# The mean and variance of a group over the partitions: one rounded pass over a high and a low half in place of a float32 product

## The chip, the cores and the metric

The kernel runs on one core of a Trainium2 chip. The metric is the time of one execution on the device, in microseconds (us), lower is better; stated is the median of the runs.

## What is computed

Two attention layers run one after the other on 16 samples of 256 channels by 2048 positions. The first layer ends in a group norm with one group: mean and variance are taken over all channels and positions of a sample. Cut to what matters here:

```
# layer 0
q, k from y; v from x
attn = softmax(q k^T / sqrt(E))               # 32 x 32 per head, over all positions
o = Wo (attn v) + bo + x
mu  = mean(o, axis=(1, 2)); var = var(o, axis=(1, 2))      # one value per sample
x1  = (o - mu) * rsqrt(var + EPS) * gn_w + gn_b
# layer 1
u = Wo1 (softmax of chunks of 64 positions of y, masked) + b
z = u + x1
out = (z - mean(z, axis=2)) * rsqrt(var(z, axis=2) + EPS)  # per channel
```

## The kernel before

Channels lie on the 128 partitions in two halves; the positions of a sample are cut into four blocks of 512. The program is written out by hand for each engine: for every sample `n` there are 16 slots `s`, and each engine runs through the slots in the order of its own `body`, with semaphores between engines. Large products run in float32r (rounded): each operand is split into a high half, which is the value rounded, and a low half, which is the rest, and `three_pass` (L313) sums three rounded products. Other products, such as the transposes (L339), are plain float32, and the trace shows each of them as two weight loads and two matmuls.

The statistics of the group norm of sample `n` are taken while `o` is made, in slots 12 to 15 (`stats_of_o`). After slot 15 of sample `n`, and across slot 0 of sample `n + 1`, they are brought together; this stretch is called the sample boundary here, and there are 15 of them, and a last one in the tail of the program. The steps are:

1. VectorE: `group_mean` (L944, L945). bn_aggr gives a mean and a variance for each partition, `o_mv`. The small copy to `carrier` ahead of it stands between the last statistics and the aggregation.
2. TensorE: `mean_over_partitions` (L489). A 128x128 matrix of 1/128 times the column of means puts the mean over the partitions on every partition, in `l0_ps[0]`. It stands behind the scores (L328) and the value products (L357) of slot 0, and ahead of the query products (L313) of the next block.
3. VectorE: `group_deviation` (L950 to L953), behind `branch` (L876), `top` (L847) and `att_low` (L871): mean copied to `o_mu`, difference squared and added to the partition's variance, `o_dev`. Behind it stands the subtraction of the row maximum, `shift` (L854).
4. TensorE: `variance_over_partitions` (L493), behind twelve query products, ahead of the transposes of the probabilities (L339).
5. VectorE: `group_variance` (L957), behind `shift`. It adds EPS and sets `gn_step`.
6. GpSimd: `group_norm` (L1137 to L1143) makes scale and shift. TensorE: the first Gram product of the next sample (`gram_part`, L424) writes the same bank of PSUM, so it waits for `gn_step` too:

```
                if q == 0:
                    if exists(n - 1, 1, 0):
                        pe.wait_ge(gn_step, count(n - 1, 1, 0))
```

In the tail the same five functions run one behind the other for sample 15; there the output product of block 2 stands behind the variance's product, and VectorE's L1100 waits for `gn_done` of GpSimd.

Of the kernel before, what the change touches and what calls it, by code (L numbers as in the profile page):

```python
# [16 lines left out]
F32R = mybir.dt.float32r  # L17
BF16 = mybir.dt.bfloat16
ALU = mybir.AluOpType
# [35 lines left out]
def build(nc, x, ctx, ctx_t, mask, w0, w1, cols, bk0, consts, out):  # L55
# [6 lines left out]
    with es:  # L62
        def sb(name, shape, dt=F32):
            return es.enter_context(nc.sbuf_tensor(name, shape, dt))
# [15 lines left out]
        c1 = sb("c1", [P, HALVES])  # L80

# [46 lines left out]
        o_dev = sb("o_dev", [P, 2])  # L128
        o_var = sb("o_var", [P, 1])
# [52 lines left out]
        power_set = sem("power_set")  # L182
        c1_done = sem("c1_done")
# [122 lines left out]
        def _(pe):  # L306
# [180 lines left out]
            def mean_over_partitions(n):  # L487
                pe.wait_ge(o_aggr, count(n, 1, 0))
                mm(l0_ps[0][:, 0:1], mean_mat, o_mv[:, 0:1], start=True, stop=True).then_inc(mean_ready, 1)  # L489

            def variance_over_partitions(n):
                pe.wait_ge(dev_done, count(n, 1, 0))
                mm(l0_ps[0][:, 1:2], mean_mat, o_dev[:, 1:2], start=True, stop=True).then_inc(var_ready, 1)  # L493
# [90 lines left out]
        def _(act):  # L584
# [145 lines left out]
            split_yt(0, 0)  # L730
            act.wait_ge(w0_in, 2 * 16)
# [91 lines left out]
        def _(dve):  # L823
# [118 lines left out]
            def group_mean(n):  # L942
                dve.wait_ge(o_stats_done, count(n, 8, 7))
                nc.vector.tensor_copy(carrier[:, 0:1], ident[:, 0:1])  # L944
                nc.vector.bn_aggr(o_mv[:, :], o_stats[:, :, :].rearrange("p a b -> p (a b)")).then_inc(o_aggr, 1)  # L945

            def group_deviation(n):
                dve.wait_ge(mean_ready, count(n, 1, 0))
                dve.wait_ge(o_aggr, count(n, 1, 0))
                nc.vector.tensor_copy(o_mu[:, :], l0_ps[0][:, 0:1])  # L950
                tt(o_dev[:, 0:1], o_mv[:, 0:1], l0_ps[0][:, 0:1], ALU.subtract).then_inc(dev_step, 1)
                dve.wait_ge(dev_step, count(n, 1, 0))
                stt(out=o_dev[:, 1:2], in0=o_dev[:, 0:1], scalar=o_dev[:, 0:1], in1=o_mv[:, 1:2], op0=ALU.mult, op1=ALU.add).then_inc(dev_done, 1)  # L953

            def group_variance(n):
                dve.wait_ge(var_ready, count(n, 1, 0))
                nc.vector.tensor_scalar(o_var[:, :], l0_ps[0][:, 1:2], EPS, None, ALU.add).then_inc(gn_step, 1)  # L957
# [281 lines left out]
```

## Time and profile before

| | |
|---|---|
| median of 3 runs | 1543.38 us (1541.15 to 1543.43) |
| the profiled execution | 1542.93 us |
| its span in the trace | 1541.1 us |
| TensorE busy | 1511.2 us, 98% of the span |
| VectorE busy | 1278.6 us, 83% |
| ScalarE busy | 1108.9 us, 72% |
| GpSimd busy | 450.8 us, 29% |
| granted TensorE clock, mean | 0.995 of 2.4 GHz |

The profile comes from one execution. PE is TensorE's matmuls and PEld its weight loads, DVE is VectorE, ACT ScalarE, POOL GpSimd. A busy share is an average over the whole program; what an operation of a sample boundary is worth is read from the rows of that boundary. Times in the timeline are in us from the start of the span, with two decimals, so a difference of two rows is good to about 0.01 us.

### The profile page before, as it was taken

What the parts mean: (1) busy time and instruction counts of PE and PEld (TensorE: products, weight loads), DVE (VectorE), ACT (ScalarE), POOL (GpSimd) and SP (SyncE); (2) the same over time, 40 slices, a digit from 0 to 9 for tenths busy, and PEclk for the clock granted to TensorE, in tenths of its full rate; (3) what the DMA queues carried; (4) which work ended last, traced back from release to release, by engine and by line L of the source; (5) the groups of instructions that cost most, each with busy time, mean ns of one, the idle gap of its engine ahead of it and who ended that gap; (6) DMA issues with size and microseconds to landing.
All of it is one profiled execution on the core that took longest, in us unless ns stands there. A gap on an engine that the chain in (4) does not pass through costs nothing.

```text
span 1541.1 us, 54826 instructions
## 1 busy us (share of the span) xinstructions
PE 1511.2 (98%) x24146; PEld 1274.8 (83%) x24146; DVE 1278.6 (83%) x2024; ACT 1108.9 (72%) x2064; POOL 450.8 (29%) x294
## 2 busy tenths in 40 slices
PE   9999999999999999999999999999999999999995
PEld 6888888888888888888888888888888888888883
DVE  5778888888788887978879888888888889788897
ACT  6667676777767777677776776867767776777765
POOL 1114133141331413314142141422314133141321
PEclk9999999999999999999999999999999999999998
DMA  7232331423315233142422414233142331524212
GB/s 250 56 99 83 111 124 38 152 84 118 111 36 152 84 118 111 54 148 71 143 86 84 132 57 145 84 111 121 55 151 78 120 116 41 149 83 129 59 49 91
DMA packets 96397, 157.28 MB, mean 102 GB/s; under 512 B 5408, under 2 KB 38304, under 8 KB 96032
## 3 DMA queue, kind: packets, MB, share of 16 engines
q1 hardware_dynamic: 96160, 153.78, 31.8%
q8 instruction: 191, 3.13, 0.8%
q14 instruction: 46, 0.38, 0.1%
HBM read 120.20 MB, written 33.55 MB: 100 GB/s over the span
## 4 chain that ended last, share of the span: by engine, by line
PE 96%; DVE 1%; ACT 1%; issue 1%; POOL 0%; ACTq 0%; POOLq 0%; DVEq 0%
PE pj_ps L313 46%; PE l_ps L313 12%; PE s_ps L328 9%; PE w_ps L339 8%; PE l_ps L424 7%; PE w_ps L357 7%; PE l_ps L441 2%; PE l_ps L468 2%; PE l_ps L462 1%; PE l_ps L471 1%; PE s_ps L499 0%; PE l_ps L450 0%; DVE o_sb L972 0%; PE l_ps L432 0%; PE l_ps L489 0%
## 5 line engine op out<-in xcount | busy, mean ns | idle before, releaser
L1132 POOL TENSOR_TENSOR prob<-prob,row_inv 128x1024 f32<-128x1024 f32 x128 | 257.9, 2015 | 890.4 <-DVE row_inv L864 890.4
L671 ACT CAST att_hi<-w_ps 128x256 fp32r<-128x256 f32 x256 | 83.2, 380 | 192.2 <-PE w_ps L357 192.1
L313 PE MATMUL pj_ps<-y_hi,w_hi 128*128 128x512 f32 x510 | 207.4, 407 | 0.0
L313 PE MATMUL pj_ps<-y_hi,w_lo 128*128 128x512 f32 x510 | 202.0, 396 | 0.0
L313 PE MATMUL pj_ps<-y_lo,w_hi 128*128 128x512 f32 x510 | 202.0, 396 | 0.0
L859 DVE TENSOR_REDUCE row_sum<-prob 128x16 f32<-128x1024 f32 x128 | 155.0, 1211 | 49.2 <-ACT prob L640 49.1
L847 DVE TENSOR_REDUCE row_max<-s_ps 128x16 f32<-128x1024 f32 x128 | 155.6, 1215 | 21.2 <-PE s_ps L328 21.2
L328 PEld LDWEIGHTS s_ps<-k_s,q_s 32*64 32x64 f32 x8192 | 130.8, 133 | 43.1 <-issue 35.2
L1149 POOL TENSOR_TENSOR o_sb<-o_sb,u_sb 128x1024 f32<-128x1024 f32 x60 | 157.7, 2638 | 0.9
L854 DVE TENSOR_TENSOR prob<-s_ps,row_max 128x1024 f32<-128x1024 f32 x128 | 155.6, 1215 | 0.1
L635 ACT COPY prob_t<-w_ps 128x512 f32<-128x512 f32 x256 | 152.2, 596 | 3.8 <-PE w_ps L339 3.1
L832 DVE TENSOR_TENSOR yt_hl<-yt_raw,yt_hl 128x1024 fp32r<-128x1024 f32 x64 | 94.8, 1482 | 70.0 <-ACT yt_hl L603 70.0
L620 ACT ACTIVATE q_s<-pj_ps,col 128x512 f32<-128x512 f32 x128 | 88.3, 690 | 89.4 <-PE pj_ps L313 88.6
L313 PE MATMUL pj_ps<-w_hi,y_hi 128*128 128x256 f32 x512 | 150.4, 294 | 0.8 <-ACT v_s L631 0.8
L339 PE MATMUL w_ps<-cst,prob 128*128 128x128 f32 x1024 | 147.8, 275 | 1.4
L328 PE MATMUL s_ps<-k_s,q_s 32*64 32x64 f32 x8192 | 148.5, 220 | 0.0
L313 PE MATMUL pj_ps<-w_hi,y_lo 128*128 128x256 f32 x512 | 144.5, 282 | 0.0
L313 PE MATMUL pj_ps<-w_lo,y_hi 128*128 128x256 f32 x512 | 144.0, 281 | 0.0
L651 ACT COPY s_ps<-blocked 128x512 f32<-128x512 f32 x256 | 143.1, 603 | 0.0
L339 PEld LDWEIGHTS w_ps<-cst,prob 128*128 128x128 f32 x1024 | 118.5, 141 | 25.9 <-issue 12.0
L640 ACT ACTIVATE prob<-prob 128x1024 f32<-128x1024 f32 x128 | 137.8, 1076 | 1.8 <-DVE prob L854 1.6
L837 DVE TENSOR_TENSOR x_lo<-x_raw,x_hi 128x1024 fp32r<-128x1024 f32 x62 | 78.8, 1271 | 62.9 <-ACT x_hi L613 62.8
(139 smaller groups left out, 3552.2 us busy)
## 6 DMA issues: line engine op xcount, KB each, us to landing
y_raw<-in_ctx SPq DMA_DIRECT2D x64, 512.0 KB, 4.9
yt_raw<-in_ctx_t SPq DMA_DIRECT2D x64, 512.0 KB, 4.6
x_raw<-in_x SPq DMA_DIRECT2D x64, 512.0 KB, 5.1
out_z<-o_sb SPq DMA_DIRECT2D x60, 512.0 KB, 3.6
mask_b<-in_mask SPq DMA_DIRECT2D x64, 256.0 KB, 4.0
out_z<-o_sb SPq DMA_DIRECT2D x8, 256.0 KB, 2.7
u_sb<-in_w SPq DMA_DIRECT2D x2, 512.0 KB, 5.8
w_sb<-in_w SPq DMA_DIRECT2D x1, 1024.0 KB, 10.7
```

The source lines that it names most:

```text
L313: last = mm(dst, lhs, rhs, start=i == 0, stop=i == len(todo) - 1)
L328: last = mm(s_ps[64 * h:64 * h + 64, r, t // 2, g, t % 2, :], q_s[rows, b % 2, g, cut], k_s[rows, b % 2, g, cut], start=False, stop=True, ...
L339: last = nc.tensor.transpose(pt_ps[:, j, 2 * g + r, :], prob[:, u % 2, r, j, g, :], ident)
L357: last = mm(av_ps[DH * i:DH * i + DH, c, g, j, :], v_s[rows, b % 2, 2 * e + j, o:o + DH], prob_t[rows, j, g, i // 2, i % 2, :], start=True ...
L635: copy(prob_t[:, j].rearrange("p g r h q -> p (g r h q)"), w_ps[:, j, :]).then_inc(pt_copied, 1)
L640: nc.scalar.activation(cut, cut, ACT.Exp, scale=SCALE1).then_inc(exp_done, 1)
L651: last = copy(s_ps[:, r].rearrange("p j g c k -> p j g (c k)"), blocked[:, b % 2, e * UT:(e + 1) * UT].rearrange("p (j t) -> p j t", j=2). ...
L847: nc.vector.tensor_reduce(row_max[:, u % 2, :], s_ps[:, :, :, :, :, :].rearrange("p r j g c k -> p (r j g c) k"), AX.X, ALU.max).then_inc( ...
L854: tt(prob[:, u % 2].rearrange("p r j g (c k) -> p (r j g c) k", c=2), s_ps[:, :, :, :, :, :].rearrange("p r j g c k -> p (r j g c) k"), ro ...
L859: nc.vector.tensor_reduce(row_sum[:, u % 2, :], prob[:, u % 2].rearrange("p r j g (c k) -> p (r j g c) k", c=2), AX.X, ALU.add).then_inc(s ...
L1132: nc.gpsimd.tensor_tensor(cut, cut, row_inv[:, u % 2, :].unsqueeze(2).to_broadcast([P, 2 * HEADS, CHUNK]), ALU.mult).then_inc(probs_done, 1)
L1149: nc.gpsimd.tensor_tensor(o_sb[:, :, cut], o_sb[:, :, cut], u_sb[:, :, cut], ALU.add).then_inc(z_done, 1)
```

## The change

The two products over the partitions become one rounded pass each. The matrix of 1/128 is copied once to float32r (`mean_r`, on ScalarE). VectorE splits the column of means into a high and a low half (`mean_hl`), TensorE multiplies both columns in one matmul of two columns, and VectorE sums the two results with a reduce. The same is done for the variance (`dev_hl`). Each new operation on VectorE waits for the one ahead of it through a semaphore of its own.

```diff
             def mean_over_partitions(n):
-                pe.wait_ge(o_aggr, count(n, 1, 0))
-                mm(l0_ps[0][:, 0:1], mean_mat, o_mv[:, 0:1], start=True, stop=True).then_inc(mean_ready, 1)
+                pe.wait_ge(mean_split, count(n, 1, 0))
+                mm(l0_ps[0][:, 0:2], mean_r[:, :], mean_hl[:, :], start=True, stop=True).then_inc(mean_ready, 1)
 
             def variance_over_partitions(n):
-                pe.wait_ge(dev_done, count(n, 1, 0))
-                mm(l0_ps[0][:, 1:2], mean_mat, o_dev[:, 1:2], start=True, stop=True).then_inc(var_ready, 1)
+                pe.wait_ge(dev_split, count(n, 1, 0))
+                mm(l0_ps[0][:, 2:4], mean_r[:, :], dev_hl[:, :], start=True, stop=True).then_inc(var_ready, 1)
...
             split_yt(0, 0)
+            act.wait_ge(consts_in, 16)
+            copy(mean_r[:, :], mean_mat)
             act.wait_ge(w0_in, 2 * 16)
...
                 nc.vector.bn_aggr(o_mv[:, :], o_stats[:, :, :].rearrange("p a b -> p (a b)")).then_inc(o_aggr, 1)
+                dve.wait_ge(o_aggr, count(n, 1, 0))
+                nc.vector.tensor_copy(mean_hl[:, 0:1], o_mv[:, 0:1]).then_inc(mean_hi_done, 1)
+                dve.wait_ge(mean_hi_done, count(n, 1, 0))
+                tt(mean_hl[:, 1:2], o_mv[:, 0:1], mean_hl[:, 0:1], ALU.subtract).then_inc(mean_split, 1)
 
             def group_deviation(n):
                 dve.wait_ge(mean_ready, count(n, 1, 0))
-                dve.wait_ge(o_aggr, count(n, 1, 0))
-                nc.vector.tensor_copy(o_mu[:, :], l0_ps[0][:, 0:1])
-                tt(o_dev[:, 0:1], o_mv[:, 0:1], l0_ps[0][:, 0:1], ALU.subtract).then_inc(dev_step, 1)
+                nc.vector.tensor_reduce(o_mu[:, :], l0_ps[0][:, 0:2], AX.X, ALU.add).then_inc(mu_done, 1)
+                dve.wait_ge(mu_done, count(n, 1, 0))
+                tt(o_dev[:, 0:1], o_mv[:, 0:1], o_mu[:, :], ALU.subtract).then_inc(dev_step, 1)
                 dve.wait_ge(dev_step, count(n, 1, 0))
                 stt(out=o_dev[:, 1:2], in0=o_dev[:, 0:1], scalar=o_dev[:, 0:1], in1=o_mv[:, 1:2], op0=ALU.mult, op1=ALU.add).then_inc(dev_done, 1)
+                dve.wait_ge(dev_done, count(n, 1, 0))
+                nc.vector.tensor_copy(dev_hl[:, 0:1], o_dev[:, 1:2]).then_inc(dev_hi_done, 1)
+                dve.wait_ge(dev_hi_done, count(n, 1, 0))
+                tt(dev_hl[:, 1:2], o_dev[:, 1:2], dev_hl[:, 0:1], ALU.subtract).then_inc(dev_split, 1)
 
             def group_variance(n):
                 dve.wait_ge(var_ready, count(n, 1, 0))
-                nc.vector.tensor_scalar(o_var[:, :], l0_ps[0][:, 1:2], EPS, None, ALU.add).then_inc(gn_step, 1)
+                nc.vector.tensor_reduce(o_var[:, :], l0_ps[0][:, 2:4], AX.X, ALU.add).then_inc(var_sum, 1)
+                dve.wait_ge(var_sum, count(n, 1, 0))
+                nc.vector.tensor_scalar(o_var[:, :], o_var[:, :], EPS, None, ALU.add).then_inc(gn_step, 1)
```

Line numbers of the changed kernel are 5 higher for TensorE's functions and 7 or more higher for VectorE's. VectorE's program at the first sample boundary, from the aggregation to the variance, before:

```order
L945 BN_AGGR o_mv<-o_stats 128x2
L876 SCALAR_TENSOR_TENSOR u_sb<-pj_ps,c,mask_b 128x512 [waits wout_ready]
L847 TENSOR_REDUCE row_max<-s_ps 128x16 [waits scores_ready]
L871 TENSOR_TENSOR att_lo<-w_ps,att_hi 128x2x2x64 [waits att_hi_done]
L871 TENSOR_TENSOR att_lo<-w_ps,att_hi 128x2x2x64
L950 COPY o_mu<-l_ps 128x1 [waits o_aggr,mean_ready]
L951 TENSOR_TENSOR o_dev<-o_mv,l_ps 128x1
L953 SCALAR_TENSOR_TENSOR o_dev<-o_dev,o_mv 128x1 [waits dev_step]
L854 TENSOR_TENSOR prob<-s_ps,row_max 128x1024 [waits transposed,max_done]
L957 TENSOR_SCALAR o_var<-l_ps 128x1 [waits var_ready]
```

The same place in the changed kernel, with the two parts that differ; the lines left out between them are those of `branch`, `top` and `att_low`, in the same order as before:

```order
L952 BN_AGGR o_mv<-o_stats 128x2
L954 CAST mean_hl<-o_mv 128x1 [waits o_aggr]
L956 TENSOR_TENSOR mean_hl<-o_mv,mean_hl 128x1 [waits mean_hi_done]
...
L960 TENSOR_REDUCE o_mu<-l_ps 128x1 [waits mean_ready]
L962 TENSOR_TENSOR o_dev<-o_mv,o_mu 128x1 [waits mu_done]
L964 SCALAR_TENSOR_TENSOR o_dev<-o_dev,o_mv 128x1 [waits dev_step]
L966 CAST dev_hl<-o_dev 128x1 [waits dev_done]
L968 TENSOR_TENSOR dev_hl<-o_dev,dev_hl 128x1 [waits dev_hi_done]
L861 TENSOR_TENSOR prob<-s_ps,row_max 128x1024 [waits transposed,max_done]
L972 TENSOR_REDUCE o_var<-l_ps 128x1 [waits var_ready]
L974 TENSOR_SCALAR o_var<-o_var 128x1 [waits var_sum]
```

Five operations are added to each boundary, two of one kind are replaced by another, and nothing changes its place. On TensorE the two products stand where they stood; before, at the second of them and the Gram product:

```order
L493 MATMUL l_ps<-o_dev,cst 128x1 [waits dev_done]
L339 MATMUL w_ps<-cst,prob 128x128 [waits att_lo_done,probs_done]
L339 MATMUL w_ps<-cst,prob 128x128 x7
L424 MATMUL l_ps<-yt_hl 128x512 [waits gn_step,yt_lo_done,yt_hi_done]
L424 MATMUL l_ps<-yt_hl 128x384
```

and in the changed kernel:

```order
L498 MATMUL l_ps<-dev_hl,mean_r 128x2 [waits dev_split]
L344 MATMUL w_ps<-cst,prob 128x128 [waits att_lo_done,probs_done]
L344 MATMUL w_ps<-cst,prob 128x128 x7
L429 MATMUL l_ps<-yt_hl 128x512 [waits gn_step,yt_lo_done,yt_hi_done]
L429 MATMUL l_ps<-yt_hl 128x384
```

Only the operands and the semaphore of the product have changed; what follows it is the same.

## Rows read from the trace of the kernel before

**Rows 1.** The page: busy time by engine, and the chain that ended last.

```profile
PE 1511.2 (98%) x24146; PEld 1274.8 (83%) x24146; DVE 1278.6 (83%) x2024; ACT 1108.9 (72%) x2064; POOL 450.8 (29%) x294
...
PE 96%; DVE 1%; ACT 1%; issue 1%; POOL 0%; ACTq 0%; POOLq 0%; DVEq 0%
```

**Rows 2.** Timeline, VectorE, first sample boundary: start, duration, engine, line, operation.

```profile
110.67 0.36 DVE L945 BATCH_NORM_AGGREGATE o_mv<-o_stats 128x2 f32<-128x48 f32 x1
...
113.34 0.15 DVE L950 COPY o_mu<-l_ps 128x1 f32<-128x1 f32 x1
113.41 0.14 DVE L951 TENSOR_TENSOR o_dev<-o_mv,l_ps 128x1 f32<-128x1 f32 x1
113.58 0.22 DVE L953 SCALAR_TENSOR_TENSOR o_dev<-o_dev,o_mv 128x1 f32<-128x1 f32 x1
...
114.86 0.15 DVE L957 TENSOR_SCALAR o_var<-l_ps 128x1 f32<-128x1 f32 x1
```

**Rows 3.** Timeline, TensorE's matmuls and weight loads, first sample boundary.

```profile
110.28 0.70 PEld L357 LDWEIGHTS w_ps<-prob_t,v_s 64*32 64x32 f32 x64
111.08 0.30 PEld L489 LDWEIGHTS l_ps<-o_mv,cst 128*128 128x128 f32 x2
111.30 0.19 PEld L313 LDWEIGHTS pj_ps<-y_hi,w_hi 128*128 128x128 f32 x1
...
113.97 0.42 PEld L493 LDWEIGHTS l_ps<-o_dev,cst 128*128 128x128 f32 x2
114.20 0.28 PE L493 MATMUL l_ps<-o_dev,cst 128*128 128x1 f32 x2
...
115.14 0.19 PEld L424 LDWEIGHTS l_ps<-yt_hl 128*128 128x128 f32 x1
```

**Rows 4.** Timeline of the tail: VectorE, TensorE's loads, GpSimd.

```profile
1516.82 0.23 DVE L953 SCALAR_TENSOR_TENSOR o_dev<-o_dev,o_mv 128x1 f32<-128x1 f32 x1
...
1517.10 0.30 PEld L493 LDWEIGHTS l_ps<-o_dev,cst 128*128 128x128 f32 x2 [0.67 <-DVE o_dev L953]
...
1519.02 0.20 POOL L1143 TENSOR_TENSOR gn<-col,gn 128x2 f32<-128x2 f32 x1
...
1519.70 0.54 DVE L1100 TENSOR_SCALAR o_sb<-o_sb,gn 128x512 f32<-128x512 f32 x1
```

**Rows 5.** Timelines of two other places where L424's load follows L357's or L832.

```profile
37.65 2.11 DVE L832 TENSOR_TENSOR yt_hl<-yt_raw,yt_hl 128x1024 fp32r<-128x1024 f32 x1 [0.95 <-ACT yt_hl L603]
...
39.88 0.70 PEld L424 LDWEIGHTS l_ps<-yt_hl 128*128 128x128 f32 x4 [0.67 <-issue]
...
120.87 0.70 PEld L357 LDWEIGHTS w_ps<-prob_t,v_s 64*32 64x32 f32 x64
121.66 1.11 PEld L424 LDWEIGHTS l_ps<-yt_hl 128*128 128x128 f32 x6
```

**Rows 6.** The tile o_mv: durations in ns (least, median, greatest), first and last start.

```profile
L489 PEld LDWEIGHTS l_ps<-o_mv,cst x32: 186/188/190, 111.1 to 1516.2; 128*128 128x128 f32 x32
```

**Rows 7.** VectorE's groups by form: busy us, mean ns, idle us before them.

```profile
L913 DVE CAST m_hi<-work_a 128x512 fp32r<-128x512 f32 x16 | 12.3, 771 | 0.5
...
L953 DVE SCALAR_TENSOR_TENSOR o_dev<-o_dev,o_mv 128x1 f32<-128x1 f32 x16 | 3.5, 220 | 0.6
...
L927 DVE TENSOR_REDUCE y_sum<-y_sums 128x2 f32<-128x8 f32 x16 | 2.4, 151 | 0.0
```

**Rows 8.** ScalarE's casts (page), ScalarE at the start and GpSimd at the boundary (timelines).

```profile
L671 ACT CAST att_hi<-w_ps 128x256 fp32r<-128x256 f32 x256 | 83.2, 380 | 192.2 <-PE w_ps L357 192.1
...
21.70 0.69 ACT L620 ACTIVATE q_s<-pj_ps,col 128x512 f32<-128x512 f32 x1 [0.98 <-PE pj_ps L313]
...
115.08 0.66 POOL L1137 TENSOR_TENSOR o_rstd<-o_var,power 128x1 f32<-128x1 f32 x1 [5.81 <-DVE o_var L957]
```

**Rows 9.** A stall of TensorE (timeline) and the stretch after it (windows: busy us, granted clock).

```profile
439.29 0.24 PE L357 MATMUL w_ps<-prob_t,v_s 64*32 64x64 f32 x1 [1.48 <-issue]
...
440.00:444.00 4.00, 4.00 (x12) 3.04 (x11) 2.74 (x8) 0.91 (x2) 0.82 (x2) 0.57 0.19 62
```

More of the change, by code:

```diff
@@ L80, in build @@
         c1 = sb("c1", [P, HALVES])
+        mean_r = sb("mean_r", [P, P], F32R)
         y_raw = sb("y_raw", [P, 2, HALVES, BT])
@@ L128, in build @@
         o_dev = sb("o_dev", [P, 2])
+        mean_hl = sb("mean_hl", [P, 2], F32R)
+        dev_hl = sb("dev_hl", [P, 2], F32R)
         o_var = sb("o_var", [P, 1])
@@ L182, in build @@
         power_set = sem("power_set")
+        mean_hi_done, mean_split, mu_done = sem("mean_hi_done"), sem("mean_split"), sem("mu_done")
+        dev_hi_done, dev_split, var_sum = sem("dev_hi_done"), sem("dev_split"), sem("var_sum")
         c1_done = sem("c1_done")
```

## The prediction

> **What bounds the kernel now.** I read the page first. TensorE is busy 98% of the span and 96% of the chain that ended last is its work [rows 1], so time is won or lost only where TensorE stands still or gets less to do. The list of TensorE's waits, which I read next, names neither of the changed products but once, in the tail. Is TensorE then far ahead of the statistics, so that they have slack, or do the two meet by chance? The list can't tell, so I went to the timeline at the first of the 15 sample boundaries.
>
> There VectorE works without an idle mark from the aggregation (L945) to L957 [rows 2]. An operation that needs nothing of the one ahead begins before its end (L951 0.08 us before L950's); L953, which waits for L951's result, starts 0.03 us after its end. TensorE's side is in [rows 3]. Two meetings are to be seen.
>
> First, L945 ends at 110.67 + 0.36 = 111.03 and the weights of the mean's product are loaded from 111.08. In the tail, where TensorE plainly waits for L953, the load at 1517.10 comes 0.05 us after VectorE's end at 1517.05 [rows 4]. So 0.05 is the reaction, and at 111.08 it is all there is. From the last value product on, TensorE needs 0.80 us from the first load of L357 to its next load; where the Gram product follows, it is 0.79 [rows 5]. TensorE gets there at most 0.01 or 0.02 us before the aggregate. The slack at the mean is zero.
>
> Second, the Gram product L424 waits for gn_step, which L957 sets. L957 ends at 114.86 + 0.15 = 115.01; L424's load is at 115.14, 0.13 later. Where L424 did wait for a semaphore of VectorE of this kind, L832 ended at 37.65 + 2.11 = 39.76 and the load came at 39.88, 0.12 later [rows 5]. The slack at the Gram product is about 0.02 us. (L424 has three waits, one of them a separate instruction, which explains the longer reaction.)
>
> Between them, the variance's product has slack: L953 ends at 113.80, the load at 113.97 would go 0.12 us earlier if it could, and its matmul starts only at 114.20, when the query products are done.
>
> The mean's product is there 16 times, the first at 111.1 and the last at 1516.2, with durations that differ by 4 ns [rows 6]: I take the 15 boundaries inside the loop as alike and the last as a case of its own.
>
> **What the change adds on VectorE, per boundary.** Every added operation depends on the one ahead of it, so each costs its duration and the 0.035 us from the end of one to the start of a dependent one: in the grouped rows the idle before L953 and L913 is 0.6 and 0.5 us over 16 of them, 0.03 to 0.04 each [rows 7]. Durations of one-column operations: copy 0.15 (L950), subtraction 0.14 (L951), L957 0.15 [rows 2]; a reduce to two columns 0.151 [rows 7]. A cast of one column from fp32 to fp32r is not in the trace; I take the copy's 0.15, bounded by 0.14 below and 0.22 (the dearest one-column row, L953) above [rows 7].
>
> - Mean: cast and subtraction, 2 x 0.035 + 0.15 + 0.14 = 0.36. L876, L847 and both L871 queue behind them and all move by 0.36.
> - Deviation: the reduce takes the copy's place (0.15 for 0.15), but the subtraction now waits for it, so it starts 0.185 after the reduce's start where it started 0.065 after the copy's: 0.12. Then cast and subtraction, 0.36. Together 0.48; the softmax subtraction L854 moves by 0.84 in all.
> - Variance: a reduce of 0.15 and the wait of 0.035 ahead of the tensor_scalar: 0.185.
>
> gn_step thus comes 0.36 + 0.48 + 0.185 = 1.03 us later at each boundary. VectorE has no idle between L945 and L957 to soak any of it up, and the order of its work isn't changed.
>
> **What it does to TensorE.** Each product loses one of its two passes: 32 loads for 16 products [rows 6]. At the mean the two loads take 111.08 to 111.30, where the next is [rows 3], so 0.11 a pass; two products save 0.22 us. But TensorE waits three times. The mean's load comes 0.36 later, less 0.11: TensorE's queries move by 0.25. The variance's load must wait for VectorE: ready 113.80 + 0.84 + 0.05 = 114.69, while TensorE would be there for its matmul at 114.20 + 0.25 = 114.45 and would have had the weights loaded by then; unhidden, the load adds some 0.11 to 114.80. So a stall of about 0.35. Then the transposes, moved by 114.80 - 114.20 - 0.11 = 0.5 in all, and the Gram product at 115.14 + 0.5 = 115.64 finds gn_step not there: it comes at 115.01 + 1.03, load at 116.16. What counts is the last of these: 1.03 - 0.02 = 1.01 us per boundary. The saved passes are inside it and worth nothing, because VectorE sets the moment.
>
> Does TensorE win it back? It has no idle to spare behind L424, and the exponentials wait for copies of the transposes, which move by 0.5 only, so the other engines have 0.5 us more room than before. Nothing else becomes late. I count 15 x 1.01 = 15.1 us.
>
> **The tail.** TensorE loads the variance's weights at 1517.10; at 1519.70 VectorE runs L1100, right behind the sum of the output product (L876) [rows 4]. Here VectorE waits for TensorE too, so the passes count: 0.36 for the mean, one pass less (0.11), 0.48 for the deviation make 0.73 at 1517.10; then one pass less, 0.62 for the output product, L876 and L1100. The other way to L1100 is GpSimd's: 0.73 + 0.185 = 0.915 on top of its end at 1519.02 + 0.20 = 1519.22 gives 1520.14, before 1519.70 + 0.62 = 1520.32. So 0.6 us.
>
> **Edits at nothing.** The new fp32r copy of the mean matrix sits on ScalarE ahead of L734, where ScalarE later idles 0.98 us before 21.70 [rows 8]; a cast twice as wide takes 0.38 (L671), so even that would be hidden, and without the idle it would cost 0.4 once. VectorE's casts could be held by GpSimd's work, but GpSimd idles 5.81 us before L1137 [rows 8]. Without this cover a cast would wait up to the end of GpSimd's operation.
>
> **Sum.** 15.1 + 0.6 = 15.7 us: span 1541.1 to 1556.8, profiled time 1542.93 to 1558.6. The median of the three runs shown, 1543.38, is 0.45 above the profiled time, so I predict 1559.1.
>
> **Rivals.** *Cheap operations*: if the added operations ran back to back at the pitch of L950 and L951, 0.065 us, they would add 5 x 0.065 = 0.33 per boundary, 0.31 after the slack: 4.7 us and 0.3 in the tail, 1548.4. Against it: L953's gap is there in every row of its kind. The Trainium skill ("VectorE: DVE Perf Modes", section "The DRAIN you can't avoid") says that a semaphore between chained operations costs nothing extra, since the pipe must empty anyway; by that this rival would be the forecast. The trace disagrees: a dependent start is 0.03 after the end, an independent one 0.08 before it. The page's rule to minimize the count of operations speaks against the change too, and there the trace agrees. Chance 0.05.
>
> *The clock falls*: at 439.29 TensorE had stood 1.48 us, and in 440 to 444 the granted clock was 0.57, most of it at the lower level of 1.2 GHz [rows 9]; 4 us x 0.43 = 1.7 us lost. Now three stalls of 0.35 to 0.5 us lie within 5 us. If that lowered the clock each time, 15 x 1.7 = 26 us more, 1585. The Trainium skill ("TensorE: Matmul & The Clock Gate", "Part 1: The HAM clock gate") has activity release a throttle that is on by default. Against it: each stall is a quarter of the one that was followed by the fall. Chance 0.04.
>
> *Faster*: if VectorE's results were early by 0.36 or more at the mean and 1.03 at gn_step, only the saved passes would show: 15 x 0.22 = 3.3 us less, 1540. It decides at those slacks; I read 0.02 at both. Chance 0.02. *Nothing*: the delay given back in each sample: 0.03.
>
> **Numbers.** Forecast 0.86. Its own range: each of seven operations 0.03 off gives 0.2 a boundary, 3 us; with all at 0.22 instead of 0.15, 7 more at the top; and the one event of 1.5 us stall and 1.7 us of clock may go or come again, 3 us. 1552 to 1565. A measurement here tells about 0.2% (3 us) from no change: slower 0.95, same 0.03, faster 0.02.
>
> **What would show it.** After: the mean's load 0.05 us after the new subtraction's end; L424's counterpart 0.12 after the variance's tensor_scalar; the distance between the mean's load of before and the Gram load, 4.06 us, becomes about 4.7, with 0.36 more ahead of it; one load and one matmul per product; VectorE busy about 16 x 0.75 = 12 us more, TensorE's busy less but its span longer. Wrong if L424 starts right behind the last transpose, or if the granted clock shows dips at each boundary.

## The result and the profile after

The changed kernel takes 1558.86 us (median of 4 runs, 1557.78 to 1560.15) against 1542.27 us of the kernel before (median of 4 runs beside it, 1541.06 to 1543.43): a ratio of 1.0108 with an interval of 1.0091 to 1.0126. It is 16.6 us slower, where 15.7 were forecast (1559.1 us). Its profiled execution took 1558.33 us, with a span of 1556.5 us.

The page of the changed kernel, busy time by engine and the chain that ended last, which answers to [rows 1]:

```profile
PE 1514.3 (97%) x24114; PEld 1270.6 (82%) x24114; DVE 1296.1 (83%) x2104; ACT 1110.8 (71%) x2065; POOL 451.0 (29%) x294
...
PE 87%; DVE 8%; ACT 3%; issue 2%; DMA 0%; ACTq 0%; POOL 0%; SPq 0%; POOLq 0%; DVEq 0%
```

TensorE has 32 matmuls fewer and VectorE 80 instructions more. The chain is the first thing to read: before, 96% of it was TensorE's; now 8% is VectorE's and 3% ScalarE's. VectorE's busy time grew by 17.5 us, not by the 12 forecast, but that number alone says nothing of the path. TensorE's busy time grew by 3.1 us, with fewer matmuls, where the prediction had it shrink.

The list of waits of the changed kernel (time in all, times, longest) now names the three places that the prediction named (the list of before had one of the two changed products, and only in the tail):

```profile
PE l_ps L494 <- DVE mean_hl L956: 5.5, 16, 0.7
...
PE l_ps L429 <- DVE o_var L974: 4.0, 15, 0.3
PE l_ps L498 <- DVE dev_hl L968: 3.8, 16, 1.1
```

The timeline of VectorE at the first boundary, which answers to [rows 2]:

```profile
109.40 1.23 DVE L839 TENSOR_TENSOR yt_hl<-yt_raw,yt_hl 128x1024 fp32r<-128x1024 f32 x1 [1.04 <-ACT yt_hl L608]
...
110.61 0.36 DVE L952 BATCH_NORM_AGGREGATE o_mv<-o_stats 128x2 f32<-128x48 f32 x1
111.00 0.15 DVE L954 CAST mean_hl<-o_mv 128x1 fp32r<-128x1 f32 x1
111.19 0.16 DVE L956 TENSOR_TENSOR mean_hl<-o_mv,mean_hl 128x1 fp32r<-128x1 f32 x1
111.27 0.74 DVE L883 SCALAR_TENSOR_TENSOR u_sb<-pj_ps,c,mask_b 128x512 f32<-128x512 f32 x1
...
113.72 0.15 DVE L960 TENSOR_REDUCE o_mu<-l_ps 128x1 f32<-128x2 f32 x1
113.90 0.16 DVE L962 TENSOR_TENSOR o_dev<-o_mv,o_mu 128x1 f32<-128x1 f32 x1
114.09 0.22 DVE L964 SCALAR_TENSOR_TENSOR o_dev<-o_dev,o_mv 128x1 f32<-128x1 f32 x1
114.35 0.15 DVE L966 CAST dev_hl<-o_dev 128x1 fp32r<-128x1 f32 x1
114.54 0.16 DVE L968 TENSOR_TENSOR dev_hl<-o_dev,dev_hl 128x1 fp32r<-128x1 f32 x1
114.62 1.22 DVE L861 TENSOR_TENSOR prob<-s_ps,row_max 128x1024 f32<-128x1024 f32 x1
115.76 0.15 DVE L972 TENSOR_REDUCE o_var<-l_ps 128x1 f32<-128x2 f32 x1
115.94 0.15 DVE L974 TENSOR_SCALAR o_var<-o_var 128x1 f32<-128x1 f32 x1
```

And TensorE's weight loads there, which answer to [rows 3]:

```profile
110.22 0.70 PEld L362 LDWEIGHTS w_ps<-prob_t,v_s 64*32 64x32 f32 x64
111.40 0.19 PEld L494 LDWEIGHTS l_ps<-mean_hl,mean_r 128*128 128x128 f32 x1 [0.48 <-DVE mean_hl L956]
...
114.75 0.19 PEld L498 LDWEIGHTS l_ps<-dev_hl,mean_r 128*128 128x128 f32 x1 [0.62 <-DVE dev_hl L968]
...
116.21 0.93 PEld L429 LDWEIGHTS l_ps<-yt_hl 128*128 128x128 f32 x5 [0.47 <-issue]
```

Each product is one load now. The mean's load at 111.40 comes 0.05 after the subtraction's end at 111.19 + 0.16 = 111.35; the variance's at 114.75 comes 0.05 after 114.54 + 0.16; the Gram load at 116.21 comes 0.12 after L974's end at 115.94 + 0.15 = 116.09. From the mean's load to the Gram load it is 4.81 us, where it was 4.06 [rows 3]. Note that the last of these stalls carries the word "issue" in the view of loads, while the list of waits puts the matmul behind it down to L974: the same stall, read in two views.

The chain that ended last, in order of time, shows the same stretch from the other side: start, duration, what.

```profile
109.40 1.23 DVE yt_hl L839
...
111.19 0.16 DVE mean_hl L956
111.35 0.66 DVE u_sb L883
...
116.24 0.87 PE l_ps L429 x3
```

It enters VectorE already at the split of `yt` (L839), ahead of the aggregation, and doesn't leave it before L974. Every operation of this stretch, small or large, is on the path.

**Steps, boundary by boundary.** To see where the time goes, matmul k of one trace was set against matmul k of the trace of before; a step is how much the distance between the two grows across a place, from the matmul ahead of it to the second one behind it. Mean over the 15 boundaries, in us:

| kernel | at the mean's product | at the variance's | at the Gram product | sum |
|---|---|---|---|---|
| changed kernel | +0.268 | +0.360 | +0.504 | +1.13 |
| changed kernel, second profile | +0.274 | +0.365 | +0.504 | +1.14 |

15 x 1.13 = 17.0 us. The rest of the difference of the spans, 15.4 us: the tail is 2.5 us longer (from the last aggregation's start to the last write of `o_sb`, 21.21 us before and 23.67 after), and between the boundaries the traces drift by -4.1 us together. Of this -3.0 is one place: the stall and the lower clock of [rows 9], which the profiled execution of before had and no other profile of this study has. In the second profile of the changed kernel (span 1559.9 us) the same account is 17.1 + 3.8 - 2.2 = 18.7 for a difference of 18.8.

### The profile page after: what moved, and what is told of

The parts are those of the page before. It is cut to its first block, busy times and chain, and to the rows that moved or that the text cites. A ratio compares the mean times of both kernels' runs of the same rounds, so it can differ in the third digit from the quotient of the medians.

```text
span 1556.5 us, 54827 instructions
## 1 busy us (share of the span) xinstructions
PE 1514.3 (97%) x24114; PEld 1270.6 (82%) x24114; DVE 1296.1 (83%) x2104; ACT 1110.8 (71%) x2065; POOL 451.0 (29%) x294
## 4 chain that ended last, share of the span: by engine, by line
PE 87%; DVE 8%; ACT 3%; issue 2%; DMA 0%; ACTq 0%; POOL 0%; SPq 0%; POOLq 0%; DVEq 0%
PE pj_ps L318 42%; PE l_ps L318 11%; PE s_ps L333 8%; PE l_ps L429 7%; PE w_ps L344 7%; PE w_ps L362 6%; PE l_ps L446 2%; PE l_ps L473 2%; DVE yt_hl L839 1%; DVE prob L861 1%; DVE row_max L854 1%; ACT yt_hl L608 1%; PE l_ps L467 1%; PE l_ps L476 1%; DVE u_sb L883 1%
## 5 line engine op out<-in xcount | busy, mean ns | idle before, releaser
L854 DVE TENSOR_REDUCE row_max<-s_ps 128x16 f32<-128x1024 f32 x128 | 155.6, 1215 | 26.5 <-PE s_ps L333 26.4
L861 DVE TENSOR_TENSOR prob<-s_ps,row_max 128x1024 f32<-128x1024 f32 x128 | 155.3, 1214 | 0.1
L839 DVE TENSOR_TENSOR yt_hl<-yt_raw,yt_hl 128x1024 fp32r<-128x1024 f32 x64 | 94.8, 1482 | 70.2 <-ACT yt_hl L608 70.2
```

The lines of the kernel that those rows point to most:

```text
L839: tt(yt_hl[:, :, 1, :], yt_raw[:, q % 2], yt_hl[:, :, 0, :], ALU.subtract).then_inc(yt_lo_done, 1)
L854: nc.vector.tensor_reduce(row_max[:, u % 2, :], s_ps[:, :, :, :, :, :].rearrange("p r j g c k -> p (r j g c) k"), AX.X, ALU.max).then_inc( ...
L861: tt(prob[:, u % 2].rearrange("p r j g (c k) -> p (r j g c) k", c=2), s_ps[:, :, :, :, :, :].rearrange("p r j g c k -> p (r j g c) k"), ro ...
```

## Experiments

The two theories that most runs set against each other: *VectorE sets the moment* (each added dependent operation costs its duration and 0.035 us, passes saved on TensorE are worth nothing), and rivals by which the cost sits on TensorE or in something else than the length of VectorE's chain.

### TensorE's part alone

The products become one rounded pass each, VectorE does what it did before. The mean's product reads a constant pair, and the variance's column is written rounded without its low half, so the statistics lack that precision and the mean is no mean. Each product still waits for the operation of VectorE that it waited for before.

```diff
-                mm(l0_ps[0][:, 0:1], mean_mat, o_mv[:, 0:1], start=True, stop=True).then_inc(mean_ready, 1)
+                mm(l0_ps[0][:, 0:2], mean_r[:, :], fix_r[:, :], start=True, stop=True).then_inc(mean_ready, 1)
...
-                mm(l0_ps[0][:, 1:2], mean_mat, o_dev[:, 1:2], start=True, stop=True).then_inc(var_ready, 1)
+                mm(l0_ps[0][:, 2:4], mean_r[:, :], dev_r[:, :], start=True, stop=True).then_inc(var_ready, 1)
```

> TensorE's part of the change alone: both products are one float32r pass of two columns, VectorE's program is that of the kernel before (the variance sum is written rounded by the operation that makes it; the mean's product reads a constant pair of columns in place of the means, so the mean is left out of the output). My theory: VectorE sets the moment of gn_step, the Gram product waits for it, and the two saved passes (0.11 us each) are worth nothing but the 0.02 us of slack: 15 x 0.02 + 0.2 in the tail = 0.5 us less than before, within the noise. Rival (a saved pass counts wherever TensorE is 98% busy): 15 x 0.22 + 0.2 = 3.5 us less. In the trace, by my theory, the Gram product's load stays 0.12 after the end of the variance's tensor_scalar, and TensorE waits 0.2 us there.

Measured: 1539.23 us against 1540.46, ratio 0.9993 (0.9984 to 1.0002). The steps are -0.113, -0.113 and +0.201, together -0.025. The loads at the first boundary:

```profile
111.15 0.19 PEld L492 LDWEIGHTS l_ps<-fix_r,mean_r 128*128 128x128 f32 x1
...
113.92 0.19 PEld L496 LDWEIGHTS l_ps<-dev_r,mean_r 128*128 128x128 f32 x1
114.16 0.85 PEld L342 LDWEIGHTS w_ps<-cst,prob 128*128 128x128 f32 x8
115.18 0.95 PEld L427 LDWEIGHTS l_ps<-yt_hl 128*128 128x128 f32 x5 [0.17 <-issue]
```

Each saved pass is worth exactly the 0.11 us read before, and both are given back at the Gram product, which now stands 0.17 us for `gn_step`. Had they counted, 15 x 0.226 = 3.4 us would have shown (a ratio of 0.9978, outside the interval). VectorE sets the moment already in the kernel before.

### VectorE's part alone

All of the change but the rounding: halves and matrix are float32, so each product is two passes again.

```diff
-        mean_hl = sb("mean_hl", [P, 2], F32R)
-        dev_hl = sb("dev_hl", [P, 2], F32R)
+        mean_hl = sb("mean_hl", [P, 2])
+        dev_hl = sb("dev_hl", [P, 2])
...
-                mm(l0_ps[0][:, 0:2], mean_r[:, :], mean_hl[:, :], start=True, stop=True).then_inc(mean_ready, 1)
+                mm(l0_ps[0][:, 0:2], mean_mat, mean_hl[:, :], start=True, stop=True).then_inc(mean_ready, 1)
```

(the variance's product alike).

> VectorE's part alone: split, reduces and all their waits as in the changed kernel, but the halves and the matrix stay float32, so each product is still two passes. My theory: the passes are hidden in the wait for VectorE, so the time is that of the changed kernel, about 16.5 us over before, plus at most 0.3 in the tail. Rival (passes count): 3.5 us more than the changed kernel, 20 us over before.

Measured: 1560.69 us against 1540.46, ratio 1.0128 (1.0115 to 1.0142), 20.2 us. The time alone would speak for passes that count. The steps don't: +0.379, +0.341, +0.410, together 1.13, the same sum as in the changed kernel, only laid out otherwise: the second pass of the mean's product shows as 0.11 more at its place and is gone at the Gram product. The surplus lies outside the boundaries, in a tail of 25.44 us (4.2 longer than before, see below) and in the drift between them. Without the trace this run would have been read wrongly.

### The variance in another bank

The prediction's third stall exists because the variance's product and the Gram product write the same bank of PSUM. Here the variance goes to a bank of the projections (`pj_ps[0]`); the Gram product no longer waits for `gn_step`, the key product of the next block does, and the variance's product waits for ScalarE's copy out of that bank.

```diff
+        def var_ps(n):
+            return pj_ps[0] if n < SAMPLES - 1 else l0_ps[0]
...
-                    if exists(n - 1, 1, 0):
-                        pe.wait_ge(gn_step, count(n - 1, 1, 0))
-                    else:
+                    if not exists(n - 1, 1, 0):
...
+                if n < SAMPLES - 1:
+                    pe.wait_ge(qkv_copied, count(n + 1, 24, 6))
                 pe.wait_ge(dev_split, count(n, 1, 0))
-                mm(l0_ps[0][:, 2:4], mean_r[:, :], dev_hl[:, :], start=True, stop=True).then_inc(var_ready, 1)
+                mm(var_ps(n)[:, 2:4], mean_r[:, :], dev_hl[:, :], start=True, stop=True).then_inc(var_ready, 1)
```

> The changed kernel with the variance's product in the bank of the query and key products (pj_ps[0]), so that the first Gram product needs not wait for gn_step; the key product, 1.6 us later, waits for it instead. My theory: the third of the three waits of a boundary (0.51 us in the changed kernel's trace) goes and nothing takes its place: 15 x 0.51 = 7.7 us less than the changed kernel, about 9 us over before. Rival (the delay is VectorE's work, and comes back at the next thing that TensorE needs from VectorE, the yt split of slot 2): no gain against the changed kernel.

Measured: 1553.73 us against 1540.46, ratio 1.0086 (1.0072 to 1.0099). Steps +0.268, +0.436, -0.001, together 0.70. The loads at the first boundary:

```profile
111.42 0.19 PEld L497 LDWEIGHTS l_ps<-mean_hl,mean_r 128*128 128x128 f32 x1 [0.48 <-DVE mean_hl L961]
...
114.83 0.19 PEld L503 LDWEIGHTS pj_ps<-dev_hl,mean_r 128*128 128x128 f32 x1 [0.68 <-issue]
114.97 0.86 PEld L347 LDWEIGHTS w_ps<-cst,prob 128*128 128x128 f32 x8
115.79 0.71 PEld L432 LDWEIGHTS l_ps<-yt_hl 128*128 128x128 f32 x4
```

The Gram load follows the transposes without a gap: the stall of 0.50 us is gone and nothing took its place. The variance's own step is 0.08 us dearer, with a second wait ahead of it; with a tail 2.1 us longer than before, this makes 12.6 us by the trace and 13.3 by the times, where about 9 were expected. So the third stall is the bank's, as the prediction had it, and the two others are the data's.

### The mean earlier

`group_mean` with its split moves ahead of the split of `yt` on VectorE, into idle time.

```diff
+                        group_mean(n)
...
-                if not last:
-                    group_mean(n)
```

> The changed kernel with the aggregation and the split of the mean moved ahead of the yt split of the next sample on VectorE, into the 1.04 us in which VectorE idles for ScalarE. My theory: all later VectorE work of the boundary comes 0.72 us earlier; the wait at the mean goes, and gn_step is 1.15 - 0.72 = 0.43 late where it was 1.15 late, so a boundary costs 0.41 in place of 1.14: 11 us less than the changed kernel, 6 us over before. Rival (each wait has a cost of its own, so only the first goes): 15 x 0.27 = 4 us less than the changed kernel.

Measured: 1549.23 us against 1540.46, ratio 1.0056 (1.0043 to 1.0068). Steps -0.125, +0.017, +0.502, together 0.39 (0.41 expected). By the times it is 8.8 us over before, where 6 were expected: the tail of this kernel is 4.0 us longer than before. VectorE at the first boundary:

```profile
108.73 0.36 DVE L952 BATCH_NORM_AGGREGATE o_mv<-o_stats 128x2 f32<-128x48 f32 x1
...
109.31 0.17 DVE L956 TENSOR_TENSOR mean_hl<-o_mv,mean_hl 128x1 fp32r<-128x1 f32 x1
109.67 1.23 DVE L839 TENSOR_TENSOR yt_hl<-yt_raw,yt_hl 128x1024 fp32r<-128x1024 f32 x1 [0.18 <-ACT yt_hl L608]
```

Ahead of the split of `yt` VectorE stood idle for 1.04 us for ScalarE in the changed kernel; now four operations of group_mean lie in that time, and the mean's product gives its saved pass as a gain (-0.125). So the 0.27 us at the mean's product was VectorE's lateness and nothing else.

### Five copies that nothing waits on, and the same five in a chain

To the kernel before are added five copies of one column near the places of the five added operations, into a tile that nobody reads. In the first kernel nothing links them; in the second each is followed by a wait of VectorE for its own semaphore. The same work, with and without dependence:

```diff
                 nc.vector.tensor_copy(carrier[:, 0:1], ident[:, 0:1])
+                nc.vector.tensor_copy(extra[:, 0:1], ident[:, 0:1]).then_inc(link, 1)
+                dve.wait_ge(link, count(n, 5, 0))
+                nc.vector.tensor_copy(extra[:, 1:2], ident[:, 0:1]).then_inc(link, 1)
+                dve.wait_ge(link, count(n, 5, 1))
```

(the other three alike; in the first kernel without `then_inc` and `wait_ge`).

> The kernel before with five more one-column copies on VectorE at each boundary that depend on nothing (two ahead of the aggregation, two ahead of the copy of the mean, one ahead of the variance's tensor_scalar). Five operations are what the change adds too, but there each waits for the one ahead. My theory: a free one-column operation costs its pitch of 0.066 us, a dependent one 0.19; gn_step comes 5 x 0.066 = 0.33 late, 0.31 after the slack, 15 x 0.31 = 4.7 us and 0.3 in the tail: 5 us over before. Rival (the count of operations sets the cost and a wait costs nothing, as the pipe empties anyway): the cost of the change without its reduces, 5 x 0.19 = 0.95 per boundary, 14 us over before.

> The kernel before with the same five one-column copies as in the run of free ones, but each operation waits for the copy ahead of it through a semaphore. My theory: 0.15 + 0.035 = 0.185 each, gn_step 0.92 late, 0.91 after the slack: 15 x 0.91 = 13.6 us, and about 1 in the tail: 14.5 over before, against 4.4 with free copies. Rival (a wait costs nothing extra): the time of the run with the free copies.

Measured, free: 1544.32 us against 1539.93, ratio 1.0027 (1.0015 to 1.0038); steps together 0.30. Chained: 1556.98 against 1541.75, ratio 1.0099 (1.0085 to 1.0113); steps +0.381, +0.140, +0.420, together 0.94. VectorE in the kernel with the free copies, behind the aggregation's place:

```profile
111.22 0.14 DVE L946 COPY extra<-cst 128x1 f32<-128x1 f32 x1
111.28 0.14 DVE L947 COPY extra<-cst 128x1 f32<-128x1 f32 x1
111.34 0.36 DVE L948 BATCH_NORM_AGGREGATE o_mv<-o_stats 128x2 f32<-128x48 f32 x1
111.61 0.68 DVE L877 SCALAR_TENSOR_TENSOR u_sb<-pj_ps,c,mask_b 128x512 f32<-128x512 f32 x1
```

and in the kernel with the chained ones:

```profile
110.80 0.14 DVE L947 COPY extra<-cst 128x1 f32<-128x1 f32 x1
110.97 0.15 DVE L949 COPY extra<-cst 128x1 f32<-128x1 f32 x1
111.16 0.37 DVE L951 BATCH_NORM_AGGREGATE o_mv<-o_stats 128x2 f32<-128x48 f32 x1
```

From one start to the next it is 0.06 us free and 0.17 to 0.19 chained. The same five copies cost 4.4 us in the one kernel and 15.2 in the other, so two thirds of the price at a boundary (0.94 less 0.30) is dependence, not work. The *cheap operations* rival of the prediction is the first of these kernels: true of operations that wait for nothing, false of the ones that this change adds. The Trainium skill ("VectorE: DVE Perf Modes", section "The DRAIN you can't avoid") has a semaphore in a chain of copies cost nothing extra. For the copies of this kernel the two runs show otherwise. The section adds that a next operation that isn't held starts earlier, and that is what the free copies do.

### The tail as before, and the change again

The changed kernel with the last sample's statistics as in the kernel before:

```diff
+                if n == SAMPLES - 1:
+                    pe.wait_ge(o_aggr, count(n, 1, 0))
+                    mm(l0_ps[0][:, 0:1], mean_mat, o_mv[:, 0:1], start=True, stop=True).then_inc(mean_ready, 1)
+                    return
```

and alike in the other four functions. It was run twice, the second time beside the changed kernel itself.

> The changed kernel with the last sample's group norm done as before (float32 products, no split), the 15 inner boundaries as changed. The trace of the changed kernel puts 2.4 us on the tail where I forecast 0.6. If the tail's share is the change's (a subtraction that ran 0.76 us beside GpSimd's 2 us operation, five dependent operations, a later stretch at the lower clock), this kernel's tail shift against before is under 0.3 us and it takes 2.1 us less than the changed kernel, about 14.5 over before. If the 2.4 is mostly chance of that execution, it takes 0.6 less.

> The changed kernel with the last sample as before, once more: its first profile had a lower mean clock over the whole run. 1.2 to 2.5 us less than the changed kernel in the same call, and from the aggregation to the last result within 0.3 us of before, if the granted clock there is as in before. If the tail's share was chance, the same time as the changed kernel.

> The changed kernel once more, to have it beside the next three on the same chip. 15 boundaries of 1.13 each and a tail of 1.2 to 4 us: 16 to 19 us over before, 1.0105 to 1.0125. In the trace the tail from the aggregation to the last result takes at least 1.2 us more than before (the dependent operations and the subtraction beside GpSimd); what is more than that comes only if the clock's lower level falls on the last output products.

Measured first: 1555.85 us against 1539.93, ratio 1.0107 (1.0094 to 1.0121). The profile of that run showed a mean granted clock of 0.945 and isn't used for steps; what its tail shows is said below. Measured again: 1559.13 against 1541.75, ratio 1.0113 (1.0099 to 1.0128), beside 1559.73 for the changed kernel, ratio 1.0120 (1.0106 to 1.0135). The two differ by 0.6 us, where 1.2 to 2.5 were expected; these few runs can't resolve it. In the traces the tail is 21.43 us in the one and 25.03 in the other, but that is one execution each, the fastest of four of the one kernel and the slowest of four of the other.

### Both moves, with the new tail and with the old

The last question is whether the whole cost can be hidden. Both moves from above (the variance in another bank, the mean earlier) are made in the changed kernel; the second kernel has the tail of before too. As a control, the two moves are made in the kernel before.

> The changed kernel with both moves, its tail as changed. Boundaries as in the run with the old tail (-0.125 at the mean, +0.09 at the variance, 0 at the Gram product, -0.08 over the sample), so all that is over before is the tail: 15 x -0.12 + 1.2 to 4 = 0 to 2 us over before. If the waits were not what the change cost, it stays well over that.

> The one-pass products with both moves of the earlier runs (aggregation and split of the mean ahead of the yt split; the variance's product in pj_ps[0] so that the Gram product waits for nothing) and the last sample as before. My theory: no wait at the mean (-0.125), about 0.09 at the variance, none at the Gram product: -0.04 per boundary and -0.08 per sample that the changed kernel's samples ran shorter; 15 x -0.12 = 1.8 us under before, at the edge of what can be told. Rival (the one-pass form costs something of its own on TensorE or VectorE whatever the waits): slower than before by 3 us or more.

> The kernel before with the same two moves alone, float32 products in two passes. The waits that the moves take away had 0.015 and 0.00 us in them, so nothing to win: 0 to 0.5 us under before. If it is faster than that, the moves and not the one-pass products are what makes the kernel with both fast.

| kernel | us | before | ratio (95%) | steps |
|---|---|---|---|---|
| changed, both moves | 1543.63 | 1541.75 | 1.0012 (1.0003 to 1.0021) | -0.126, +0.118, +0.001 |
| changed, both moves, old tail | 1539.02 | 1539.93 | 0.9993 (0.9984 to 1.0002) | -0.12, +0.08, 0 (medians) |
| before, both moves | 1539.61 | 1539.93 | 1.0002 (0.9993 to 1.0011) | -0.014, -0.005, -0.001 |

With both moves the boundaries cost nothing, and the kernel with the old tail stands level with the one before; it isn't shown to be faster. (One of its 15 boundaries has a step of +0.40 at the mean's product, and three have one of -0.11 to -0.12 at the variance's, unexplained.) The moves alone give nothing either, so they didn't pay for the change: they took it off the path. Between the first two rows the ratios differ by 0.0019, some 3 us (each stands beside its own runs of the kernel before, so this is the weaker sort of comparison): the price of the tail.

## Why the prediction came out as it did

The forecast was 15.7 us, and 16.6 were measured, 18.0 in the second comparison. Its mechanism was right at each boundary; the tail, a small term, was wrong in kind. That the sum came so close is in part luck. By the traces the boundaries cost 17.0 us where 15.1 were forecast and the tail 2.5 where 0.6 were, 3.8 us more together. Most of it is made up by the event of [rows 9], worth 3.0 us: the prediction's base has it, and the changed kernel's profile doesn't. The prediction had allowed for that in its range, but not in its sum.

**Slack.** "The slack at the mean is zero" and "the slack at the Gram product is about 0.02 us": both held. With VectorE's part alone the mean's product came 0.379 later, all that VectorE was late there. In the run with TensorE's part alone, 0.226 us saved ahead of the Gram product was given back as 0.201.

**Three waits of TensorE.** Forecast 0.25, some 0.25 more at the transposes (0.5 in all), and 1.01 at the Gram product; in steps +0.25, +0.25, +0.51. Measured +0.27, +0.36, +0.50. The 0.11 that the forecast lacks at the variance's product is about what VectorE was later there than forecast (0.38 + 0.06 + 0.52 = 0.96 measured, 0.84 forecast; the terms are below). TensorE's loads stood 0.48, 0.62 and 0.47 us at the three places, a third of the 1.48 us of [rows 9] and more; the prediction called them a quarter.

**The sum at a boundary.** 1.01 forecast, 1.13 measured in steps, and the terms can be read in the timelines above:

| term | forecast | measured | from |
|---|---|---|---|
| mean: cast and subtraction | 0.36 | 0.38 | 111.35 less the aggregation's end at 110.61 + 0.36 |
| `u_sb` behind them | 0 | 0.06 | 0.74 for L883, against 0.68 where it stands right behind the aggregation |
| deviation | 0.48 | 0.52 | steps of the starts from L960 to L861 against L950 to L854 |
| variance | 0.185 | 0.18 | 115.94 less 115.76 |
| sum, less 0.02 of slack | 1.01 | 1.12 | |

The terms that were mis-sized are the first three. The subtraction takes 0.159 us and not 0.14: it was priced with the row of a subtraction that reads PSUM and writes float32 [rows 2]. The cast, which no row of before showed, takes 0.153 against the 0.15 taken and the bounds of 0.14 and 0.22. And `u_sb` lost a small advantage that no step of the prediction had: right behind the aggregation it takes 0.68 us (the row of the kernel with free copies), anywhere else 0.74 (mean 741 ns over its 128 in the changed kernel). An inserted operation can so make its neighbour dearer.

**"Does TensorE win it back?"** Not at the boundary, as forecast. Between the boundaries the first profile of the changed kernel drifts by -0.05 to -0.10 us in the five of the 14 stretches between them that no larger step hides; the second profile of the same kernel, in the same five, by -0.03 to +0.02. It differs between executions of one kernel, so it isn't the change's, and what it is stays open.

**The copy of the matrix.** ScalarE's added cast was put at nothing, and costs nothing: the aggregation of the first boundary starts at 110.61, not later than the 110.67 of before.

**The tail** is the step that failed: 0.6 us forecast, 2.5 in one profile and 3.8 in the other. VectorE at the end of the changed kernel:

```profile
1529.03 0.15 DVE L954 CAST mean_hl<-o_mv 128x1 fp32r<-128x1 f32 x1
1529.21 0.76 DVE L956 TENSOR_TENSOR mean_hl<-o_mv,mean_hl 128x1 fp32r<-128x1 f32 x1
```

GpSimd beside it:

```profile
1528.05 1.90 POOL L1149 TENSOR_TENSOR prob<-prob,row_inv 128x1024 f32<-128x1024 f32 x1 [9.06 <-DVE row_inv L871]
```

The tile of the split, least, median and greatest duration in ns, says that this happens once in 16:

```profile
L954 DVE CAST mean_hl<-o_mv x16: 153/153/154, 111.0 to 1529.0; 128x1 fp32r<-128x1 f32 x16
L956 DVE TENSOR_TENSOR mean_hl<-o_mv,mean_hl x16: 158/159/757, 111.2 to 1529.2; 128x1 fp32r<-128x1 f32 x16
```

The subtraction takes 757 ns instead of 159 and ends at 1529.97, just when GpSimd's operation does (1528.05 + 1.90 = 1529.95). The prediction wrote of its cover for the boundaries that "without this cover a cast would wait up to the end of GpSimd's operation", and didn't look whether the tail has the cover. It hasn't; but what waits is the subtraction, with two operands in SBUF, and not the cast, which ran beside the same operation in 0.15 us. All six profiles with the new tail show it (752 to 757 ns, its end 0.02 us behind the end of GpSimd's operation). The trace of before had the same hold in a row of [rows 5]: L832 of VectorE, also with two operands in SBUF, takes 1.22 us at 109.47, with GpSimd idle, and 2.11 at 37.65, where it began inside this operation of GpSimd:

```profile
36.78 1.90 POOL L1132 TENSOR_TENSOR prob<-prob,row_inv 128x1024 f32<-128x1024 f32 x1 [8.21 <-DVE row_inv L864]
```

GpSimd ends at 38.68, and L832 1.08 us later, at 39.76. The price of the tail's missing cover could be read there.

Up to the first write of `x1` (L1117) the changed kernel needs 1.24 us more than before from the aggregation on: the 0.62 forecast and the 0.60 of the hold. The rest comes behind it, and the clock falls there. Two windows of the tail, 3 to 8 and 8 to 12 us behind the last aggregation's start; the third number from the end is the granted clock. The changed kernel:

```profile
1531.60:1536.60 5.00, 3.29 (x79) 2.58 (x78) 4.60 (x11) 2.73 (x6) 1.12 (x4) 1.00 0.01 3
1536.60:1540.60 4.00, 3.38 (x9) 2.70 (x10) 2.84 (x6) 3.93 (x6) 0.00 (x0) 0.57 0.00 0
```

The kernel before:

```profile
1518.70:1523.70 5.00, 2.67 (x77) 2.13 (x76) 4.60 (x9) 4.00 (x8) 0.39 (x2) 1.00 0.01 3
1523.70:1527.70 4.00, 2.38 (x11) 1.58 (x9) 3.76 (x10) 2.66 (x4) 0.03 (x1) 1.00 0.00 0
```

In the second window of the changed kernel TensorE runs the last products of the program for part of the time at the lower level of 1.2 GHz. The matmuls around the fall, in the changed kernel:

```profile
1530.03 0.27 PE L494 MATMUL l_ps<-mean_hl,mean_r 128*128 128x2 f32 x1 [0.65 <-DVE mean_hl L956]
1531.38 0.27 PE L498 MATMUL l_ps<-dev_hl,mean_r 128*128 128x2 f32 x1 [1.08 <-DVE dev_hl L968]
...
1531.83 0.40 PE L318 MATMUL pj_ps<-att_lo,w_hi 128*128 128x512 f32 x1
...
1537.22 0.77 PE L318 MATMUL pj_ps<-att_hi,w_hi 128*128 128x512 f32 x1 [1.60 <-ACT att_hi L676]
1537.78 0.63 PE L318 MATMUL pj_ps<-att_lo,w_hi 128*128 128x512 f32 x1
```

TensorE stands 0.65 and 1.08 us for the two products (before: none and 0.58) and, as before, twice more behind them; and the same matmul that takes 0.40 us at 1531.83 takes 0.63 at 1537.78. In the eight profiles of kernels with added operations in the tail, the granted clock falls to 0.5 between 2.7 and 9.0 us behind the last aggregation, and the tail takes 22.5 to 25.4 us. In five with the tail of before (before, TensorE's part alone, the moves alone, two with the old tail) it is 1.00 for 12 us, and the tail takes 21.2 to 21.4 us. The sixth with the old tail is the profile with the mean granted clock of 0.945: its clock was 0.949 all along, fell to 0.5 after 7.7 us, and its tail took 22.5 us. So the rival *the clock falls* was placed where it didn't come. At the boundaries, with stalls of about 0.5 us, the granted clock is 1.00 in every one; in the tail it fell within 9 us in eight of eight profiles with added operations and in one of six without.

That a longer chain is what brings the fall isn't shown. With the five free copies the first write of `x1` comes only 0.09 us later than before, and the clock fell; with the old tail in the changed kernel it comes 0.21 us later, and in two of three profiles the clock didn't fall within 12 us. Each profile is one execution, and the moment moves between executions of one kernel (8 us behind the aggregation in one profile of the changed kernel, 4 in the other). Which stall does it, or what else, stays open.

**The other rivals.** *Faster* is excluded by the run with TensorE's part alone, *nothing* by the time, *cheap operations* by the pair of kernels with five copies. The prediction took this rival for the forecast by the sentence of the Trainium skill on the semaphore ("VectorE: DVE Perf Modes", section "The DRAIN you can't avoid"), and that is not what the sentence gives: where a semaphore costs nothing because the pipe empties anyway, the free copies would cost what the chained ones do, some 14 us. They cost 4.4.

**What would have shown it.** Reaction of 0.05 and 0.12 us: seen. The distance of 4.7 us from the mean's load to the Gram load: 4.81, with 0.38 ahead of it. VectorE's busy time grew by 17.5 us where about 12 was written. That estimate had 0.75 us of added operations per boundary; five of them at 0.155 make 12.4, L883's 0.06 makes 1.0 and the hold 0.6. The other 3.5 us are not accounted for, and the number is no measure of the path either way. TensorE's busy time was forecast to shrink and grew by 3.1 us; 1.6 of it lies in the two windows of the tail above, the rest is open.

## What to carry to other kernels

Before a TensorE pass is traded for small operations of VectorE, find out whose end sets the moment of the product: here a saved pass was worth 0.11 us on TensorE and nothing in time, and a one-column VectorE operation cost 0.19 us in a chain and 0.06 outside one. An engine that shows few waits can still be met exactly by another; read the reaction time (0.05 and 0.12 us here) where a wait is certain, and compare the close meetings with it. And cost the tail by its own timeline: what holds inside the loop (GpSimd idle, TensorE's clock) may be missing there.

## What had not been expected of the hardware

- A subtraction of one column, SBUF with SBUF, was held from 0.159 to 0.757 us until an operation of GpSimd ended (in six profiles of six), while a cast of one column beside the same operation took its usual 0.153.
- An operation that waits for the one ahead starts 0.02 to 0.04 us after its end, an independent one some 0.08 before it. That adds up to 15.2 against 4.4 us for the same 80 copies.
- The same operation (`u_sb`, 128x512) takes 0.68 us right behind an aggregation and 0.74 elsewhere.
- In the tail the granted clock fell to its lower level within 9 us in eight of eight profiles with added small operations, and in one of six without. The added work is small (0.09 us up to the first write of `x1` with the free copies, 1.24 in the changed kernel, the hold included), and what brings the fall isn't shown.
- A profile can differ by 3 us in a place that the change doesn't touch: a stall named "issue" with the lower clock behind it [rows 9] stood in one of 14 profiles, the one of before.
